# Moving two norms' moments to GpSimd and reordering three engine queues in a fused attention and spiking feed-forward kernel

## The reference, cut to what matters

```python
x = x + layernorm(attn(layernorm(x)))      # norm 1 inside, norm 2 outside
x = x + layernorm(ffn(layernorm(x)))       # norm 3 inside, norm 4 outside
# attn: q, k, v = x @ W_qkv.T;  k is normalised per head
#   F = retention * F + coef * outer(v_t, k_t);  y_t = (W_LTM + F) @ q_t;  out = y @ W_o.T
# ffn: y = relu(x @ W_fc.T)**2 @ W_proj.T; five leaky integrate-and-fire steps
#   driven by the constant y; the mean number of spikes (0 to 5) is the output
```

## Time and profile before

| what | value |
|---|---|
| median of 3 runs | 610.22 us (607.24 to 612.72) |
| the profiled execution, its own time | 610.32 us |
| its span, first to last instruction | 608.5 us |
| DVE busy | 555.7 us, 91% |
| PE busy | 491.8 us, 81% |
| POOL busy | 383.0 us, 63% |
| ACT busy | 312.0 us, 51% |
| granted TensorE clock, mean | 0.902 |

### The profile page before, as it was taken

How to read it: one execution, slowest core, us unless ns; L and a number is a source line. 1 busy time by engine, 2 the same in 40 slices (tenths; PEclk the granted TensorE clock), 3 DMA queues, 4 the chain that set the end, 5 groups by cost and what they waited for, 6 DMA issues and landing times.

```text
span 608.5 us, 7825 instructions
## 1 busy us (share of the span) xinstructions
PE 491.8 (81%) x2273; PEld 323.3 (53%) x2282; DVE 555.7 (91%) x974; ACT 312.0 (51%) x615; POOL 383.0 (63%) x183
## 2 busy tenths in 40 slices
PE   3774566458997899969996999789996999698985
PEld 2442134225575566736673657556663667365764
DVE  6779999998999999999999999899999999992665
ACT  4422322343537655577646753665556744664452
POOL 1027985587557876687668776687668776754010
PEclk9678577758999799979997998979997999999998
DMA  7556576556464577338744566357732876500101
GB/s 247 151 144 155 138 175 171 138 163 166 133 179 109 145 195 210 119 104 228 196 130 139 164 190 166 102 134 197 216 113 71 234 206 165 139 19 1 34 6 64
DMA packets 54778, 87.64 MB, mean 144 GB/s; under 512 B 5456, under 2 KB 19408, under 8 KB 54736
## 3 DMA queue, kind: packets, MB, share of 16 engines
q1 hardware_dynamic: 54160, 87.12, 52.4%
q10 hardware_dynamic: 576, 0.03, 0.1%
HBM read 78.74 MB, written 8.39 MB: 143 GB/s over the span
## 4 chain that ended last, share of the span: by engine, by line
PE 55%; POOL 13%; issue 12%; ACT 10%; DVE 8%; DMA 1%; ACTq 0%; POOLq 0%; DVEq 0%
PE p_c L365 13%; PE p_c L390 13%; POOL prod L1197 10%; PE p_a L300 7%; PE p_y L343 6%; PE p_c L356 3%; ACT sign L676 3%; DVE state L944 3%; PE p_a L320 2%; PE p_c L373 2%; PE p_y L338 2%; POOL x1t L1213 2%; PE p_u L517 1%; PE p_c L382 1%; ACT hr L654 1%
## 5 line engine op out<-in xcount | busy, mean ns | idle before, releaser
L1197 POOL TENSOR_TENSOR prod<-state,qf 128x1024 f32<-128x1024 f32 x128 | 303.1, 2373 | 149.5 <-DVE state L944 125.9
L944 DVE TENSOR_TENSOR_SCAN state<-ret,p_u 128x512 f32<-128x512 f32 x256 | 309.2, 1208 | 0.0
L934 DVE TENSOR_TENSOR p_u<-vrep,p_k 128x512 f32<-128x512 f32 x256 | 171.4, 675 | 3.3 <-ACT p_k L598 3.3
L365 PE MATMUL p_c<-wproj_sb,ht 128*128 128x256 f32 x448 | 102.8, 382 | 0.3 <-ACT ht L656 0.3
L300 PE MATMUL p_a<-xt,wqkv_s 128*128 128x512 f32 x276 | 85.2, 449 | 12.7 <-DVE kf L926 3.2
L365 PEld LDWEIGHTS p_c<-wproj_sb,ht 128*128 128x128 f32 x448 | 83.4, 190 | 22.4 <-issue 10.1
L390 PE MATMUL p_c<-x1t,wfc_s 128*128 128x512 f32 x336 | 84.2, 402 | 5.6 <-POOL x1t L1213 5.5
L343 PE MATMUL p_y<-prod,summer 128*32 128x512 f32 x512 | 75.8, 668 | 8.4 <-POOL prod L1197 8.4
L300 PEld LDWEIGHTS p_a<-xt,wqkv_s 128*128 128x128 f32 x276 | 54.7, 208 | 47.7 <-issue 17.4
L390 PEld LDWEIGHTS p_c<-x1t,wfc_s 128*128 128x128 f32 x336 | 63.3, 191 | 22.8 <-POOL x1t L1213 8.6
L654 ACT ACTIVATE hr<-p_c 128x512 f32<-128x512 f32 x56 | 33.4, 597 | 26.0 <-PE p_c L390 24.4
(11 more groups left out here) (164 smaller groups left out, 584.9 us busy)
## 6 DMA issues: line engine op xcount, KB each, us to landing
vrep<-v_rows SPq DMA_DIRECT2D x256, 256.0 KB, 3.7
xa<-in_x SPq DMA_DIRECT2D x9, 512.0 KB, 5.6
v_rows<-vf SPq DMA_DIRECT2D x16, 256.0 KB, 2.1
x<-in_x SPq DMA_DIRECT2D x7, 512.0 KB, 5.0
out<-x SPq DMA_DIRECT2D x7, 512.0 KB, 3.4
ht<-in_w_fc SPq DMA_DIRECT2D x1, 1024.0 KB, 7.3
wproj_sb<-in_w_proj SPq DMA_DIRECT2D x1, 1024.0 KB, 9.9
state<-in_w_qkv SPq DMA_DIRECT2D x1, 512.0 KB, 5.5
```

The costliest lines, as they stand in the source:

```text
L365: last = pe.matmul(p_c[(u + 1) % 2][:, 0:D], ht[:, f, tokens(u)], wproj_sb[:, f, :], start=(f == 0), stop=(f == FT - 1))
L934: v.tensor_tensor(p_u[n % NU][:, :], vrep[:, n % NV, :], p_k[:, :], ALU.mult).then_inc(S["hebb_done"], 1)
L944: v.tensor_tensor_scan(state[:, s % NS, i, :], ret[:, r:r + 1].broadcast_to([P, L]), p_u[n % NU][:, :], 0.0, ALU.mult, ALU.add).then_inc(S ...
L1197: p.tensor_tensor(prod[:, s % NZ, :, :], state[:, s % NS, :, :], qf[:, s // HS, :].unsqueeze(1).broadcast_to([P, 2, L]), ALU.mult).then_in ...
```

## The change

1. GpSimd computes the variance of norms 1 and 4 from the bn_stats output: `moments_of` there, five small tensor_tensor on 128x4 for norm 1 and six for norm 4, with three waits for its own results in between. DVE's bn_aggr for these two norms goes, except for sequence 0. `deviation` scales by 1/256 on the way. `spike_offsets` moves from four DVE tensor_scalar to two GpSimd tensor_tensor with one wait.
2. `turn_x1` writes p_a, and p_a is shared with the projections by new waits. The second spike count moves from slot 9, ahead of x1's transposes, to slot 10 behind `project_v(b, 0)`; its signs move on ACT from ahead of x1's copies to behind them. Norm 4's statistics move on DVE from slot 10 to 11, its reciprocal from 12 to 13; on ACT its deviation moves to slot 12, its application to slot 14, and POOL's `add_feed_forward` from slot 13 to 15.
3. `turn_x(b, 0)` moves ahead of `down(b2, 3)` on PE; on ACT `copy_key(g, 1)` moves ahead of `deviation(3, b1)` and `copy_xt(b, 0)` behind it. Norm 1's deviation moves to slot 2, its reciprocal and application to slot 3. `key_variance(b, 0)` moves from slot 12 to between two `up` of slot 11, `key_deviation(b, 0)` from slot 12 to slot 11.
4. At the end: in iteration 7 `sums(7, 5)` now runs ahead of `count_last` and `down(6, 0)`; ACT's last `copy_y` runs ahead of norm 4's deviation; the first `tail_signs` runs ahead of norm 4 of sequence 6 on ACT and ahead of its reciprocal on DVE.

The diff, cut to what is spoken of:

```diff
...
     def project_v(b, half):
...
         pe.wait_ge(S["k_done"], at(2 * b + half))
+        if half == 0: pe.wait_ge(S["x1t_done"], at(KT * (b - 1)))
...
     def project_k(b, half):
...
     def turn_x1(b, t):
         pe.wait_ge(S["n3_done"], at(TILES * (b + 1)))
-        pe.wait_ge(S["o_done"], at(2 * (b + 1)))
-        pe.wait_ge(S["spk_done"], at(2 * (b - 1) + t + 1))
+        pe.wait_ge(S["k_done"], min(2 * (b + 2), 2 * B))
+        pe.wait_ge(S["xt_done"], min(KT * (b + 3), KT * B))
+        pe.wait_ge(S["x1t_done"], at(KT * b + t))
         for u in range(TILES):
-            last = pe.transpose(p_c[(t + 1) % 2][:, tokens(u)], oo[:, u, t * P:(t + 1) * P], ident_sb[:, :])
+            last = pe.transpose(p_a[:, tokens(u)], oo[:, u, t * P:(t + 1) * P], ident_sb[:, :])
...
     def up(b, f):
...
         pe.wait_ge(S["relu_done"], at(FT * b + f - 1))
+        if b == LAST - 1 and f == 1:
+            pe.wait_ge(S["yf_done"], TILES * b)
+        elif f < 2:
+            pe.wait_ge(S["spk_done"], at(2 * (b - 1) + f + 1))
...
         last.then_inc(S["up_done"], 1)
-    def turn_x1_last(t):
...
     def count_last():
...
             if now and s == 5: key_scale(g, 1)
+            if after and s == 6: turn_x(b, 0)
...
             if after:
-                if s in (6, 7): turn_x(b, s - 6)
+                if s == 7: turn_x(b, 1)
...
                 if s == 11: project_k(b, 0)
-                if s == 12: key_variance(b, 0)
...
                 if s == 14: key_scale(b, 0)
-            if two_before and s in (8, 9) and after: count_spikes(b2, s - 8)
-            if before and after and s == 9:
+            if two_before and s == 8: count_spikes(b2, 0)
+            if two_before and after and s == 10: count_spikes(b2, 1)
+            if before and s == 9:
...
                 turn_x1(b1, 1)
+            if after and not before and s == 11: key_variance(b, 0)
...
                 if s == 10: up(b1, 0)
-                if s in (11, 13):
-                    up(b1, s - 10)
-                    up(b1, s - 9)
+                if s == 11:
+                    up(b1, 1)
+                    key_variance(b, 0)
+                    up(b1, 2)
+                if s == 13:
+                    up(b1, 3)
+                    up(b1, 4)
...
                 if s == 15:
...
             if not after:
-                if s == 8: count_spikes(b2, 0)
-                if s == 9:
-                    turn_x1_last(0)
-                    turn_x1_last(1)
...
                     up(b1, 2 * (s - 10) + 1)
-                if s == 13:
+                if s == 14:
...
                     down(b1, 0, False)
-                if s == 14: down(b1, 1, False)
+                if s == 15: down(b1, 1, False)
...
     def deviation(n, b):
         act.wait_ge(S[f"n{n}_var"], at(b + 1))
-        eps = eps_sb[:, 1:2] if n == 4 else eps_sb[:, 0:1]
-        nc.scalar.activation(dev[n - 1][:, :], moments[n - 1][:, :, 1], ACT.Sqrt, bias=eps).then_inc(S[f"n{n}_dev"], 1)
+        if n in (1, 4):
+            eps = eps_sb[:, 1:2] if n == 4 else eps_sb[:, 0:1]
+            nc.scalar.activation(dev[n - 1][:, :], squares[n][:, :], ACT.Sqrt, bias=eps, scale=1.0 / D).then_inc(
+                S[f"n{n}_dev"], 1)
+        else:
+            nc.scalar.activation(dev[n - 1][:, :], moments[n - 1][:, :, 1], ACT.Sqrt, bias=eps_sb[:, 0:1]).then_inc(
+                S[f"n{n}_dev"], 1)
...
     def norm4(b):
-        act.wait_ge(S["n4_step"], at(2 * (b + 1)))
+        act.wait_ge(S["n4_offset"], at(b + 1))
...
     def copy_x1t(b, t):
         act.wait_ge(S["x1t_low"], at(KT * (b - 1) + t + 1))
-        copy(p_c[(t + 1) % 2][:, :], x1f[:, t, :], "x1_turned", KT * b + t + 1, "x1t_done")
+        copy(p_a[:, :], x1f[:, t, :], "x1_turned", KT * b + t + 1, "x1t_done")
...
     def hidden(b, f):
...
             if s == 0:
                 if now and before: copy_key(g, 0)
-                if after: deviation(1, b)
...
             if s == 1:
...
             if s == 2:
+                if after: deviation(1, b)
...
                 if now: key_deviation(g, 1)
-                if after: norm1(b)
...
                 if now: copy_q(g, 1)
+                if after: norm1(b)
...
             if s == 6:
-                if after: copy_xt(b, 0)
...
             if s == 7:
+                if now: copy_key(g, 1)
                 if before: deviation(3, b1)
+                if after: copy_xt(b, 0)
             if s == 8:
-                if now: copy_key(g, 1)
...
                 if before: norm(3, b1, x1[b1 % 2], oo, "x1_done", b1 + 1)
-                if two_before and after: signs(b2, 1)
-            if s == 9 and after:
-                if two_before:
-                    copy_count(b2, 0)
-                    copy_count(b2, 1)
+            if s == 9:
+                if two_before: copy_count(b2, 0)
...
                     copy_x1t(b1, 1)
-            if s == 9 and not after:
-                copy_count(b2, 0)
-                copy_x1t_last(0)
-                copy_x1t_last(1)
-                signs(b2, 1)
+                if two_before: signs(b2, 1)
             if s == 10:
                 if after: copy_v(b, 0)
+                if two_before and after: copy_count(b2, 1)
...
             if s == 11:
                 if now: copy_y(g, 0)
-                if two_before and after: deviation(4, b2)
...
                 if before and after: hidden(b1, 1)
+                if after: key_deviation(b, 0)
...
                 if not after: hidden(b1, 3)
-            if s == 12:
-                if not after:
-                    hidden(b1, 4)
-                    hidden(b1, 5)
-                if after: key_deviation(b, 0)
-                if two_before and after: norm4(b2)
+            if s == 12 and two_before and after: deviation(4, b2)
+            if s == 12 and not after:
+                hidden(b1, 4)
+                hidden(b1, 5)
...
                     copy_count_last()
+            if s == 14 and two_before and after: norm4(b2)
...
+    copy_y(LAST, 1)
     deviation(4, LAST - 2)
-    copy_y(LAST, 1)
...
     deviation(4, LAST - 1)
+    tail_signs(0)
     norm4(LAST - 1)
-    tail_signs(0)
...
+    def moments_of(n, b):
         dve.wait_ge(S[f"n{n}_stats"], at(b + 1))
-        dve.wait_ge(S[f"n{n}_step"], at(b if n < 4 else 2 * b))
+        dve.wait_ge(S[f"n{n}_step"], at(b))
...
         v.reciprocal(rdev[n - 1][:, :], dev[n - 1][:, :]).then_inc(S[f"n{n}_step"], 1)
-    def spike_offsets(b):
-        dve.wait_ge(S["n4_step"], at(2 * b + 1))
-        for u in range(TILES):
-            last = v.tensor_scalar(nmr[:, u:u + 1], moments[3][:, u, 0:1], rdev[3][:, u:u + 1], -1.0, ALU.mult,
-                                   ALU.mult)
-        last.then_inc(S["n4_step"], 1)
...
     def mean_out():
...
             if g == 0 and s == 0: statistics(1, b, xa, "x_in", 16 * (b + 1))
-            if after and s == 2: scales(1, b)
+            if after and s == 3: scales(1, b)
             if now and s == 4: key_reciprocal(g, 1)
-            if before and s == 4: statistics(2, b1, oo, "o_done", 2 * (b1 + 1))
+            if before and s == 4:
+                statistics(2, b1, oo, "o_done", 2 * (b1 + 1))
+                moments_of(2, b1)
...
             if now and s == 6: norm_k(g, 1)
-            if before and s == 7: statistics(3, b1, x1[b1 % 2], "x1_done", b1 + 1)
-            if two_before and after and s == 10: statistics(4, b2, spk, "spk_done", 2 * (b2 + 1))
-            if two_before and after and s == 12:
-                scales(4, b2)
-                spike_offsets(b2)
+            if before and s == 7:
+                statistics(3, b1, x1[b1 % 2], "x1_done", b1 + 1)
+                moments_of(3, b1)
+            if two_before and after and s == 11: statistics(4, b2, spk, "spk_done", 2 * (b2 + 1))
+            if two_before and after and s == 13: scales(4, b2)
...
     scales(4, LAST - 2)
-    spike_offsets(LAST - 2)
...
     statistics(4, LAST - 1, spk, "spk_done", 2 * LAST)
+    tail_signs(0)
     scales(4, LAST - 1)
-    spike_offsets(LAST - 1)
-    tail_signs(0)
...
          "wv_low")
+    steps = [0]
+    def step(ins):
+        steps[0] += 1
+        ins.then_inc(S["pool_step"], 1)
+        pool.wait_ge(S["pool_step"], steps[0])
+    def moments_of(n, b):
+        pool.wait_ge(S[f"n{n}_stats"], at(b + 1))
+        pool.wait_ge(S[f"n{n}_dev"], at(b))
+        means = [stats[n - 1][:, :, i] for i in (1, 4)]
+        sums = [stats[n - 1][:, :, i] for i in (2, 5)]
+        if n == 4:
+            p.tensor_tensor(twice_mean[:, :], means[0], means[1], ALU.add)
+        p.tensor_tensor(squares[n][:, :], sums[0], sums[1], ALU.add)
+        step(p.tensor_tensor(spread[n][:, :], means[0], means[1], ALU.subtract))
+        step(p.tensor_tensor(spread[n][:, :], spread[n][:, :], eight[:, :], ALU.mult))
+        step(p.tensor_tensor(spread[n][:, :], spread[n][:, :], spread[n][:, :], ALU.mult))
```

(29 more changed lines are left out.)

16 lines of the change are left out of this document (2 added, 14 removed).

## The result

The changed kernel takes 590.0 us in the median (587.19 to 592.93), the kernel before beside it 608.73, ratio 0.968 [0.961, 0.976]. My 595.5 had the sign right and the size too small, and what it said bounds the loop was wrong; the time lies 1 us under the range. Run again on another chip the changed kernel took 592.2 to 595.6, median 593.6, ratio 0.972 [0.969, 0.976]. (One more execution there, of 960 us, was disturbed; it and its profile, the only one of that run, stand in no number here.)

What follows compares the result with a forecast made beforehand. The prediction took DVE's queue plus its waits to bound the loop. Loop gains of 13.65 us and drain gains of 1.2, together 14.85, off the profiled 610.32 gave 595.5 us; eight-in-ten range 591 to 603.

Steps and rivals of the forecast that it cites:

- Aggregates and offsets off DVE: DVE in the loop: 0.42 us each for norms 1 and 4, and 0.61 for the offsets, saved per iteration.
- Slot 8: DVE's reciprocal, late because of ACT, no longer waits in slot 8: 0.83 us in iterations 2, 3, 4 and 6.
- the key wait: DVE's key reciprocal in slot 13 no longer waits, key variance running earlier: 0.34 us; 2.28 in iteration 1.
- The new wait at `scales(4)`: DVE in slot 13 would wait for ACT's norm 4 deviation: 0.80 us lost per iteration, between 0.47 and 1.6.
- the 0.8 of cover: Slot 11: the second spike count would be ready for norm 4's statistics with 0.8 us to spare, so no wait.
- Iteration 5: Its longer slot-8 wait, from slower PE, also goes: 1.68 us beyond the usual 1.82, 3.5 in all.
- Iteration 1: Norm 1's aggregates (0.42 us) and the longest key wait with its restart (2.28) go: 2.7 gained.
- Drain: After the loop: tail starts 0.55 us earlier, last spikes 0.65 earlier; together 1.2, bounds 0 and 2.
- Dear small operations: Rival: GpSimd's 128x4 operations cost 1.28 us each, time 608, no change to speak of; 0.10 with no change.
- slower, by the clock: Rival: PE at low clock makes the slot 13 wait 6.5 us per iteration, time 624; chance 0.05.
- stall in slot 8 stays: Rival: key copy still finds ACT busy, 5.8 us less gain, time 601; 0.22 shared with removed work only.
- Removed work only: Rival: waits return elsewhere, only DVE's own work of 8.1 us is gained, time 602; 0.22 shared with slot 8 kept.

Runs made afterwards that it cites:

- bank alone: Kernel before with x1's transposes in the projection bank and the changed kernel's counts, signs, norm 4 places and drain, other orders old, moments on DVE: ratio 1.002.
- the removed work alone: Kernel before with only moments of norms 1 and 4 and offsets on GpSimd, norm 1's deviation and reciprocal later: 617.68 us, ratio 1.012.
- the single orders: Kernel before with only the slots 6 to 8 order, only the earlier key variance, or only the bank, counts and drain: ratios 0.996, 1.001, 1.002.
- all orders: Changed kernel with aggregates and offsets put back on DVE, all new queue orders kept: 597.53 us, ratio 0.979.

## Why the forecast was right in its sign and too small

- *What bounds the kernel.* "So in the loop the time is DVE's queue, instruction by instruction, plus what it waits" is the step that failed, though the loop's sum came out. What set the iteration was a cycle of 65.2 us outside DVE: 1.7 us more in a group of PE cost 1.8, 0.98 less in the count gave 1.0, while 0.41 more of work on DVE cost PE no wait, and 1.44 less of it gained nothing. DVE's own work was 64.4, and its waits filled the rest, wherever they stood. That the cycle runs over PE, ACT and POOL as drawn above is a reading that adds up to the iteration; bank alone went against one link of it. My terms came out only because the change makes all of them at once, and this is luck: the removed work alone costs 1.2%, the single orders give 0.4% at most.
- *Aggregates and offsets off DVE*, 0.42 + 0.42 + 0.61 = 1.45: DVE's work per iteration fell from 64.13 (all orders) to 62.80, 1.33.
- *Slot 8* (0.83) *and the key wait* (0.34): both gone. They gave 1.1 together, with the bank, and not one by one.
- *The new wait at `scales(4)`*, taken at 0.80 between 0.47 and 1.6: 0.31 to 0.40, in iterations 2, 5 and 6. From `up` 0 on the clock was full in all of them. In iterations 3 and 4 the statistics waited for spk instead, 0.35 and 0.98, the case that I named as wrong, so the 0.8 of cover failed twice; in iteration 4 `project_v` and the count ahead of `up` 0 ran at half clock (2.93 and 2.36), in iteration 3 nothing there did. Against a forecast of 1.82 each, iterations 2, 3, 4 and 6 gave 1.86, 2.16, 1.55 and 2.13, and this term is most of the 0.4 that they have over the sum.
- *Iteration 5*: the slow PE stretch was in `project_out`. In the changed kernel's iteration 5 these sixteen matmuls were slow again (5.24 in the chain of waits, 5.39 in the timeline), and cost nothing:

```profile
350.73 5.24 PE p_c L362 x16
```

  The same group took 5.39 in the timeline of the kernel before, and DVE waited 1.91 behind it. So the change also buys indifference to the clock: iterations of 66.9 to 69.0 stand in the profiles of seven of the ten kernels that lack a part of the order; in the seven that have all of it the longest is 64.9.
- *Iteration 1*: 1.68 for 2.7, since a wait for the key's scale, 0.94, took a part of the kdev wait's place.
- *Set-up and iteration 0*: the sum had 0.42. `osum` took 2771 ns in the kernel before and 169 after. I had read only the loop and the drain for instructions held by POOL. With the key variance behind the sums it was 2.72 to 2.80 in six kernels of six; ahead of them POOL idles at that moment, and it was 0.17 in six of eight. This is a gain of the change, in most executions. The Trainium skill, in SBUF — State Buffer, Who interferes with whom, says that an instruction that can't get the shared port pair stands still for the whole of the other side's instruction. The 2771 ns agree with a side that stands still, but reach over more than one instruction: DVE came 0.9 into a product and went on 0.02 behind the end of the next POOL operation, and so in all eight profiles in which it was held.

```profile
84.48 2.77 DVE L916 TENSOR_SCALAR osum<-osum 128x2 f32<-128x2 f32 x1
...
83.58 2.40 POOL L1197 TENSOR_TENSOR prod<-state,qf 128x1024 f32<-128x1024 f32 x1
85.92 1.31 POOL L1213 TENSOR_TENSOR wfc_s<-ht,wfc_s 128x512 fp32r<-128x512 f32 x1
```

- *The start* (3.55) is not the change's: the first kf comes at 29.3 to 33.6 us in the eleven profiles of kernels that lack a part of the change, mean 31.8, and at 29.4 to 33.4 in the six others, mean 31.5.
- *Drain*: 0.55 forecast ahead of the tail. 2.22 in this pair; 0.7, 0.7, 0.8 and -0.5 in the other four profiles with the moments and the new drain. The executions differ by the clock: the first 24 `up` matmuls of iteration 7 took 5.85 us here and 7.35 before. In the two of the four where they took 7.40 the gain is 0.7, so 0.55 was about right at the same clock and some 1.5 of this pair is luck. At the end 1.32 for 0.65: this term was mis-sized, the new order gives 1.4 there in every profile.
- *Range*: without the start the profiled pair gives 19.5, as the medians do (18.7). Of that 13.0 are in the loop (13.2 forecast), 3.0 in iteration 0 (0.42), 3.5 in the drain (1.2): these last two terms and the start, which the sum had at nothing, are what put the time under the range. I had 0.03 for "a better drain and clock than counted", and the drain's upper bound of 2 and nothing for iteration 0 set the low end. The 593.6 of the second chip lies inside the range. *Dear small operations* (0.20 measured), *slower by the clock* and *stall in slot 8 stays* did not come. *Removed work only* came in part: the waits did come back in every version with the moments and without the whole order, and took all of the removed work.

## What to carry to other kernels

A busy engine with small waits in every iteration of a steady loop may still be a passenger: lay the cycle over the other engines down before you add up what is taken off the busy one, and test it with a little useless work on that engine. The trace may hold the test already: where a group on another engine took longer once, see whether the iteration grew by as much. Edits that each cut one of several links of such a cycle are worth nothing, or less, one at a time; judge them together. And look for a short instruction with a long duration anywhere in the trace, not just where the change is.

## Not expected of the hardware

- A tensor_scalar on DVE of two columns took 2.72 to 2.80 us beside POOL's products and 0.17 without: more than one POOL instruction (2.37), up to the end of the second of two that ran back to back. Nothing in the loop, with one input in PSUM, was held.
- The same 128x4 operations on POOL cost 0.16 us back to back and 0.28 with a wait for the one before.
- Sixteen matmuls of 256 columns took 3.62 to 3.72 us, and 5.17 to 5.41 with half of the granted clock in a part of them; this came behind an idle of 2.3 us in the tail and of 1.4 us (with light work behind it) in `project_out`. The same 1.4 stand ahead of `project_out` in iteration 4 of the kernel before, where it took 3.70, and 2.33 stand ahead of the tail's first sixteen both in the changed kernel (3.72) and with all orders (5.41), so the idle just ahead does not decide it alone.
